# One unit of an attention kernel in another order: both halves of a query tile, then the weights' product

## The reference, cut to what matters

```python
# B = 8, S = 256, E = 1024, 32 query heads, 8 key heads of 128, float32
x = x + xattn(layernorm(x), ctx, ctx, pos, mask, Wq, Wk, Wv, Wo)
x = x + ffn(layernorm(x), qweight, qzeros, scales, bias)

def xattn(query, key, value, position_ids, src_mask, Wq, Wk, Wv, Wo):
    q, k, v = heads(query @ Wq), heads(key @ Wk), heads(value @ Wv)
    q = q * cos + rotate_half(q) * sin
    k = k * cos + rotate_half(k) * sin
    scores = where(mask == 0, -1e9, q @ k.T / sqrt(128))
    return (softmax(scores) @ v) @ Wo
```

## Time and profile before

| | |
|---|---|
| median of 3 runs | 2278.1 us (2277.42 to 2279.24) |
| the profiled execution | 2282.69 us, its span 2280.9 us |
| Tensor busy | 2227.9 us, 98% |
| Vector busy | 1376.6 us, 60% |
| Scalar busy | 1057.6 us, 46% |
| Pool busy | 1383.0 us, 61% |
| chain that ended last | Tensor 81%, Pool 5%, Vector 5%, transfers 4% |

### The profile page before, as it was taken

How to read it: one execution, slowest core, us unless ns; L and a number is a source line. 1 busy time by engine, 2 the same in 40 slices (tenths; PEclk the granted TensorE clock), 3 DMA queues, 4 the chain that set the end, 5 groups by cost and what they waited for, 6 DMA issues and landing times.

```text
span 2280.9 us, 33313 instructions
## 1 busy us (share of the span) xinstructions
PE 2227.9 (98%) x10562; PEld 1866.8 (82%) x10562; DVE 1376.6 (60%) x2535; ACT 1057.6 (46%) x2296; POOL 1383.0 (61%) x981
## 2 busy tenths in 40 slices
PE   8999999999999998899999999799999999999999
PEld 6888887888888887688888888678788888888887
DVE  4772574777777777677777777523777245453432
ACT  3232133767666765667666666523334333331000
POOL 1320554788888887688888888565564354364210
PEclk9999999999999999999999999999999999999999
DMA  6766674677788878778787788588555465452111
GB/s 249 267 223 221 240 254 166 207 238 243 244 250 248 246 246 255 239 233 248 240 254 243 247 252 250 157 308 283 188 185 165 147 198 156 154 191 83 47 47 47
DMA packets 300779, 476.71 MB, mean 209 GB/s; under 512 B 23552, under 2 KB 195872, under 8 KB 300704
## 3 DMA queue, kind: packets, MB, share of 16 engines
q1 hardware_dynamic: 286624, 440.12, 60.2%
q10 hardware_dynamic: 13312, 33.56, 3.7%
q0 software_dynamic: 768, 2.10, 0.3%
HBM read 303.70 MB, written 171.98 MB: 209 GB/s over the span
## 4 chain that ended last, share of the span: by engine, by line
PE 81%; POOL 5%; DVE 5%; DMA 4%; issue 3%; ACT 2%; SPq 1%; POOLq 0%; ACTq 0%; DVEq 0%
PE ps L238 19%; PE ps L240 18%; PE ps L239 18%; PE ps L781 8%; PE ps L782 8%; PE ps L783 8%; DMA sq_scratch<-scores 3%; POOL s_buf L1519 1%; POOL q_t L1579 1%; POOL rope_tmp L1519 1%; SPq L440 1%; POOL q_t L1568 1%; PE ps L805 1%; DVE rope_tmp L1134 1%; ACT wq_t L849 1%
## 5 line engine op out<-in xcount | busy, mean ns | idle before, releaser
L238 PE MATMUL ps<-act_t,wq_t 128*128 128x512 f32 x1280 | 502.0, 392 | 16.5 <-DVE act_t L1195 9.4
L239 PE MATMUL ps<-act_t,wq_t 128*128 128x512 f32 x1280 | 500.9, 391 | 0.0
L240 PE MATMUL ps<-act_t,wq_t 128*128 128x512 f32 x1280 | 499.1, 390 | 0.0
L1597 POOL TENSOR_TENSOR b_parts<-wraw,b_parts 128x512 fp32r<-128x512 f32 x112 | 197.8, 1766 | 267.0 <-ACT b_parts L997 267.0
L781 PE MATMUL ps<-b_parts,a_parts 128*128 128x512 f32 x896 | 349.7, 390 | 3.4 <-DVE rows L1414 1.9
L1579 POOL TENSOR_TENSOR q_t<-pt_raw,q_t 128x1024 fp32r<-128x1024 f32 x124 | 298.9, 2410 | 86.7 <-ACT q_t L975 85.2
L782 PE MATMUL ps<-b_parts,a_parts 128*128 128x512 f32 x896 | 348.9, 389 | 0.0
L783 PE MATMUL ps<-b_parts,a_parts 128*128 128x512 f32 x896 | 348.8, 389 | 0.0
L1302 DVE TENSOR_TENSOR a_parts<-xring,a_parts 128x1024 fp32r<-128x1024 f32 x112 | 148.7, 1328 | 304.9 <-ACT a_parts L992 304.9
L992 ACT ACTIVATE a_parts<-xring 128x1024 fp32r<-128x1024 f32 x112 | 118.9, 1062 | 391.5 <-PE ps L783 387.4
L238 PEld LDWEIGHTS ps<-act_t,wq_t 128*128 128x128 f32 x1280 | 241.7, 189 | 65.9 <-DVE act_t L1195 10.4
(11 more groups left out here) (131 smaller groups left out, 4372.2 us busy)
## 6 DMA issues: line engine op xcount, KB each, us to landing
sq_scratch<-scores SPq DMA_DIRECT2D x124, 512.0 KB, 4.7
pt_raw<-sq_scratch SPq DMA_DIRECT2D x496, 128.0 KB, 3.1
xring<-left_scratch SPq DMA_DIRECT2D x112, 512.0 KB, 3.9
left_scratch<-s_buf SPq DMA_DIRECT2D x64, 640.0 KB, 4.9
wraw<-in_L_xattn_Wq SPq DMA_DIRECT2D x64, 512.0 KB
wraw<-in_L_xattn_Wo SPq DMA_DIRECT2D x64, 512.0 KB, 4.8
v_scratch<-kv_t ACTq DMA_DIRECT2D x32, 512.0 KB, 3.2
k_scratch<-kv_t ACTq DMA_DIRECT2D x32, 512.0 KB, 5.0
```

Of the source, the lines that this page charges most:

```text
L238: eng.matmul(dst, lh, rh, start=(k == first), stop=False)
L239: eng.matmul(dst, lh, rl, start=False, stop=False)
L240: mm = eng.matmul(dst, ll, rh, start=False, stop=(k == last))
L1597: pool.tensor_tensor(b_parts[:, s % 2, 1, :], wraw[s % 2][:, 0:NW], b_parts[:, s % 2, 0, :].bitcast(F32), ALU.subtract).then_inc(right_lo, 1)
```

## The change

In each unit of the attention, instructions are put in another order on five engines. None is added or removed.

- Tensor: `query` half 0, `query` half 1, `weigh`, instead of `weigh` between the halves.
- Scalar: `scaled` ahead of `turned_hi`, instead of behind it.
- Vector: `out_copy` at the start of a unit, ahead of `query_rot`, and of one unit further back (u8 - 3); before, it stood ahead of `inverse_sum` at the end, for u8 - 2.
- Pool: `rope_sum`, `turned_lo`, `query_lo`, `combine`, instead of `turned_lo`, `rope_sum`, `combine`, `query_lo`.
- Sync: `load_turned` ahead of `store_sums`.

```diff
@@ sync
                     if not (first and qq < 0):
                         if u8 % 2 == 0:
                             store_outputs(G * 4 + qq, G * 2 + qq // 2, qq % 2)
-                        else:
-                            store_sums(G * 4 + qq, G * 2 + qq // 2, qq % 2)
                     if not tail:
                         load_turned(G, u8, first=first and u8 < 2)
+                    if u8 % 2 == 1 and not (first and qq < 0):
+                        store_sums(G * 4 + qq, G * 2 + qq // 2, qq % 2)
@@ tensor
                     query(pair, i, 0, G * UPG + (u8 + 4))
+                    if switch and u8 in (4, 6):
+                        pe.wait_ge(next_lo, 2 * (u8 - 4) + 4)
+                    query(pair, i, 1, G * UPG + (u8 + 4))
                     if u8 >= 2:
                         weigh(G, u8 - 2, fresh=first and u8 < 4)
                     elif not first:
                         weigh(G - 1, UPG + u8 - 2)
-                    if switch and u8 in (4, 6):
-                        pe.wait_ge(next_lo, 2 * (u8 - 4) + 4)
-                    query(pair, i, 1, G * UPG + (u8 + 4))
@@ scalar
                         exponents(nG, nxt)
-                    if last and u8 <= 4 or not last:
+                    if not tail:
+                        scaled(nG, nxt)
+                    if not (last and u8 > 4):
                         if u8 > 0:
                             turned_hi(G, u8 - 1, first=first and u8 < 3)
...
-                    if not (last and u8 == UPG - 1):
+                    if tail and u8 < UPG - 1:
                         scaled(nG, nxt)
@@ vector
                     tail = last and u8 >= 4
+
+                    if u8 >= 3 and not (last and u8 >= 5):
+                        out_copy(G, u8 - 3, fresh=first and u8 < 7)
+                    elif u8 < 3 and not first:
+                        out_copy(G - 1, UPG + u8 - 3)
                     if not (last and u8 >= 5):
...
-                    elif u8 >= 2:
-                        out_copy(G, u8 - 2, fresh=first and u8 < 6)
-                    elif not first:
-                        out_copy(G - 1, UPG + u8 - 2)
                     if not (last and u8 == UPG - 1):
                         inverse_sum(nG, nxt)
@@ gpsimd
                 for u8 in range(UPG):
+                    if not (last and u8 >= 5):
+                        rope_sum(rope_tmp, q_rot, G * UPG + (u8 + 4), q_sum)
                     if not (last and u8 >= 6):
                         if u8 >= 2:
                             turned_lo(G, u8 - 2)
                         elif not first:
                             turned_lo(G - 1, UPG + u8 - 2)
                     if not (last and u8 >= 5):
-                        rope_sum(rope_tmp, q_rot, G * UPG + (u8 + 4), q_sum)
+                        query_lo(TILES[(u8 + 3) % 4], G * UPG + (u8 + 3))
                     qq = (u8 - 4) // 2
                     if not (first and qq < 0):
                         combine(G * 4 + qq, qq % 2, u8 % 2, fresh=first and qq == 0)
-                    if not (last and u8 >= 5):
-                        query_lo(TILES[(u8 + 3) % 4], G * UPG + (u8 + 3))
```

## The result

The changed kernel takes 2343.7 us (median of 4 runs, 2342.5 to 2350.6) against 2278.2 us before (2277.4 to 2279.2): ratio 1.029, 95% interval 1.0277 to 1.0303. It is 65.6 us slower. The forecast was 2306.5 with a range to 2326: the right direction, less than half of the loss. The profiled run of the changed kernel is the slowest of the four (2350.6 us, span 2348.8), 6.9 us above the median, so the sums read from its trace are somewhat too large for the typical run.

The account below looks back on a forecast made before the run. Tensor was taken as the bound, at 8.26 us a regular unit. 24.9 + 1 + 5 - 2.5 = +28.4 us on the profiled 2282.7 gave 2311.1, less 4.6 to the median: 2306.5 us, range 2287 to 2326.

Parts of the forecast that it names:

- the tiles' own chain: Steps within a regular unit, from W's end through copy, rotation, sum and splits to the next W or S.
- closed loop: W, copy, rotation, sum, turned split, next W: 6.80 against 6.90 us; charged 0 to 0.03 in some 88 units, 1 us.
- the head's split held behind the turned split: Vector's weight-head split asks at 5.44, waits for Pool's turned split, runs 6.67 to 7.76 and holds Pool's query split.
- 28 x 0.89 = 24.9 us: At b = 0 the next S starts 0.79 us late and takes 0.10 longer, in 28 units: +24.9 us.
- The order at the port: At the shared SBUF port, waiting Vector goes before Pool's next instruction; rival that Pool goes first: +26 us, chance 0.04.
- the collision: Vector's head split and Pool's splits contending for the SBUF port, delaying S at b = 0: +24.9 us.
- the loop is the bound: Rival: copy, rotation, sum and turned split take 0.05 to 0.25 us more, +4 to +22, 2311 to 2328; chance 0.2.
- the store is issued later in turn: Sync's store of sums, issued some 3 us into the next unit, lands at about 8, where Pool wants the buffer.
- Cost nothing: Charge for Sync's reordered transfers: nothing, or at the other end 0.2 us in half of the units, 12 us.
- the change of halves: Between batch halves: W behind two waits, 2.7 us, and store of sums up to 2.9 later; taken +5, bounds 2.7 and 8.
- W moved behind waits: At the change of halves W used to run inside two long query waits and now follows them: 2 x 1.36 = 2.7 us.
- Gains: Tensor's waits for Pool's query split outside the change of halves and b = 0, at most 3.7 us, can go: -2.5.

Follow-up runs that it names:

- e11: e8 with Vector's split of the next query head cut to one column (other low parts left out): 2293.3 us, ratio 1.0072.
- e8: The changed kernel with the stores of the sums issued from Scalar's queue instead of Sync's, at units with even u8: 2307.8 us, ratio 1.0127.
- e14: The changed kernel with the store of the sums still on Sync, but directly behind the next unit's store of the squares: 2311.1 us, ratio 1.0126.
- e10: The kernel before with Pool's sums of outputs behind the split of the queries and their stores issued from Scalar's queue: 2293.3 us, ratio 1.007.
- e6: The kernel before with Tensor's new order alone: 2289.0 us, ratio 1.0043.
- e1: The changed kernel with Sync's old order put back, the store of the sums ahead of the load of the turned weights: 2332.1 us, ratio 1.0239.
- e15: e8 plus a 4 KB transfer that waits for nothing, in the changed kernel's slot for the store on Sync's queue: 2311.8 us, ratio 1.0126.

## Why the prediction was wrong

**Right: the tiles' own chain.** Every link of the closed loop, the head's split held behind the turned split, and Vector served ahead of Pool's next instruction. Forecast 28 x 0.89 = 24.9 us. The profile has 27 such waits of 0.54 us, and the two kinds of unit lose 22.3 us, 20.5 more than before. In the unit shown, the next scores start 0.73 late and take some 0.09 longer, 0.82 against 0.89; the row says 0.54, since it counts from the end of the last matmul, 0.39 long, while such matmuls start 0.23 apart. The order at the port held: the head's split takes 2.27 us, and the query split that it holds as well. The Trainium skill (SBUF — State Buffer, section "Who interferes with whom") has the first to issue keep the shared pair of ports for its whole instruction. With 2.27 for 1.30 the trace agrees. It shows besides that Vector, waiting, goes ahead of Pool's next. e11 against e8 prices the collision at 12.5 to 14.5 us in the time.

**Right: the loop.** Charged 1 us. In e8, where nothing disturbs it, units without a collision lose 5.8 us, with 1.7 before. The rival "the loop is the bound" isn't what happened, but its last clause, "a late store of sums", names the cause.

**Wrong: "the store is issued later in turn, some 3 us into the next unit, and its 4.9 us to land end at about 8". "Cost nothing, at the other end 0.2 us in half of the units, 12 us."** This is the step that failed. The landing was right, 3.9 to 5.2 us. The issue was not: 3.4 us in one unit of four, and 5.2, 5.5 and 7.3 in the others. I took Sync's place in time from the trace of before and moved one instruction in it, as if Sync had slack. It had 15.4 us in the whole stage, and the moved issue left a wait and went into work. The cost was 37 us, put at nothing in the sum: the changed kernel against e8, each against before. That is the difference between forecast and result (37.2 us). I had the threshold nearly right (7.92 or 8.92 for Pool's want of the buffer, with Pool's slack 9.8), and did not ask what is late if it is passed.

**Mis-sized: the change of halves.** Forecast +5, bounds 2.7 and 8; it was +13.0 in the profiled execution, the slowest of four, so partly perhaps that execution's own. In e8 it is +0.9. So the part that I named first, W moved behind waits, cost about 1 us and not 2.7, and the other, the store of the sums ahead of the loads, about 12. I bounded it by how late the sums would be for one store; the delay went round Sync's and Pool's loops, and the store just ahead of this stretch held Pool's sum for 6.3 us and so W for 4.0.

**Gains.** The S waits outside b = 0 are gone, as forecast, -2.5 to -3.7, too small to check apart.

Together: the forecast was 28.4 us over before; e8 and e14 took 28.4 and 29.8. That agreement is partly luck. In the trace of e8 the collision is worth 20.5 us and not 24.9, the loop 4.1 and not 1, the change of halves 0.9 and not 5, and 0.7 lie in the last units (4.4 in e14), which the forecast had not.

Left open: the 16 us of e10 and the 9.6 of e6; what the 640 KB add in the slot; and how much of the 24 us by which e1 lies above e8 is the late squares (in the profiled executions 16.6 us of it lie in the change of halves). The new orders of Scalar and Vector were not run alone; with all orders but Sync's in place, units without a collision lose 5.8 us in e8.

## What to carry to other kernels

A queue that only issues transfers is an engine: count its round, issues and waits, against the unit, before moving anything in it. An issue inside a wait for a landing took nothing from the round here (slack 173.3 us in e14); behind it, even 4 KB took 31 of 51.0 us of slack (e15). When a store frees a buffer, work out the latest landing that harms nobody, and what stands behind the instruction that waits for it, on its engine and on the next ones. Two halves of a move can each be bad alone and need a third edit; here another queue, or a place behind the next store.

## What the runs showed of the hardware

The same 512 KB store of squares took a median of 5.0 us from issue to landing in the changed kernel, 4.7 before, and 3.4 in e14 (the list of issues in the profile of e14):

```profile
sq_scratch<-scores SPq DMA_DIRECT2D x124, 512.0 KB, 3.4
```

In e14 it is issued with 2.6 other transfers in flight on average, in the other two with 3.9. Within e14 the mean landing is 2.8 us where one other is in flight (22 stores), 3.1 with two (29), 3.8 with three (34) and 4.9 with four (20). So the wait that Sync sees also depends on what is still on its way, and in this stage Sync itself had issued all of it. I had counted issues and taken the landing as given. Slack alone does not bring the shorter landing: e8, with 51.0 us of it and 4.0 in flight, has a median of 4.9.
